# A graph network on one core: a shorter last destination block, scales taken ahead, column statistics beside the additions

## The reference, cut to what matters

```python
def _sage_bn_relu(h, src, dst, Wl, bl, Wr, gamma, beta):
    agg = segment_sum(h[src], dst, num_segments=N)
    deg = segment_sum(ones, dst, num_segments=N)
    mean_agg = agg / maximum(deg, 1.0)[:, None]
    out = mean_agg @ Wl + bl + h @ Wr
    mu = out.mean(axis=0); var = out.var(axis=0)
    out = (out - mu) * rsqrt(var + EPS) * gamma + beta
    return relu(out)
h = layernorm(x)
for params in three_layers:        # widths 256 -> 512 -> 512 -> 256
    h = _sage_bn_relu(h, src, dst, *params)
x = x + h
...
```

## Time and profile before

| what | value |
|---|---|
| median of 3 runs | 3179.72 us (3179.55 to 3182.9) |
| the profiled execution | 3180.59 us, span of its instructions 3178.8 us |
| TensorE (PE) busy | 2346.3 us, 74% |
| TensorE weight loads (PEld) busy | 1819.8 us, 57% |
| VectorE (DVE) busy | 1310.3 us, 41% |
| GpSimd (POOL) busy | 908.5 us, 29% |
| ScalarE (ACT) busy | 410.4 us, 13% |
| mean granted TensorE clock | 0.863 |

### The profile page before, as it was taken

The page is one execution under the profiler, slowest core; times in us unless marked ns, Lnnn a source line. Parts: engine busy times, 40 slices in busy tenths (PEclk is TensorE's granted clock), DMA queues, the critical chain, the costliest instruction groups (busy, mean ns, idle before and its releaser), DMA issues.

```text
span 3178.8 us, 40745 instructions
## 1 busy us (share of the span) xinstructions
PE 2346.3 (74%) x14330; PEld 1819.8 (57%) x14330; DVE 1310.3 (41%) x2751; ACT 410.4 (13%) x822; POOL 908.5 (29%) x643
## 2 busy tenths in 40 slices
PE   1122100058858999998996977999899995999997
PEld 1111100035636776776773455888688874888886
DVE  6599999954422011112116834113311775111111
ACT  0011000000005200004102213000200001322322
POOL 2588888888800000000002210000100000333332
PEclk6556555579979999999997969999999986999998
DMA  9833333367660699960251000444244424666665
GB/s 353 294 43 52 48 46 53 40 207 254 159 219 14 153 234 277 202 178 0 94 186 37 0 0 0 145 146 154 73 132 147 143 76 137 187 189 180 192 189 135
DMA packets 288646, 426.61 MB, mean 134 GB/s; under 512 B 166210, under 2 KB 223833, under 8 KB 288511
## 3 DMA queue, kind: packets, MB, share of 16 engines
q1 hardware_dynamic: 104959, 297.03, 28.9%
q10 hardware_dynamic: 109696, 106.77, 12.0%
q0 software_dynamic: 73936, 22.14, 8.0%
HBM read 307.61 MB, written 100.96 MB: 129 GB/s over the span
## 4 chain that ended last, share of the span: by engine, by line
PE 58%; DVE 7%; issue 3%; ACT 3%; DMA 1%; POOL 1%; DVEq 1%; ACTq 0%; SPq 0%
PE ps L1561 14%; PE ps L1778 7%; PE ps L1779 7%; PE ps L1856 7%; PE ps L1847 7%; PE ps L1499 4%; PE ps L1578 3%; PE ps L1729 1%; PE ps L1628 1%; PE ps L1756 1%; ACT harena L822 1%; DVE harena L1150 1%; DVE harena L1149 1%; DMA odd_counts<-harena 1%; DVE harena L1148 1%
## 5 line engine op out<-in xcount | busy, mean ns | idle before, releaser
L1778 PE MATMUL ps<-harena,ring 128*128 128x257 f16 x2500 | 555.3, 274 | 3.8 <-DVE harena L1237 2.7
L1779 PE MATMUL ps<-harena,ring 128*128 128x256 f16 x2500 | 554.9, 273 | 0.0
L1561 PE MATMUL ps<-ring,harena 128*128 128x320 f16 x4000 | 553.3, 301 | 1.9 <-issue 1.0
L1561 PEld LDWEIGHTS ps<-ring,harena 128*128 128x128 f16 x4000 | 393.6, 98 | 159.0 <-issue 3.6
L513 POOL DMA_INDIRECT at_counts<-harena x224 | 357.9, 1598 | 147.7 <-issue 66.7
L977 DVE SCALAR_TENSOR_TENSOR late<-ring,ps 128x1024 f16<-128x1024 f32 x312 | 379.0, 1276 | 2.7 <-issue 2.7
L1553 PE MATMUL ps<-ring,ones 128*128 128x320 f16 x250 | 44.7, 333 | 385.7 <-DVE ring L1057 385.7
L513 POOL DMA_INDIRECT odd_counts<-harena x192 | 307.6, 1602 | 60.3 <-issue 59.3
L1778 PEld LDWEIGHTS ps<-harena,ring 128*128 128x128 f16 x2500 | 242.8, 97 | 43.3 <-DVE harena L1281 3.9
L1779 PEld LDWEIGHTS ps<-harena,ring 128*128 128x128 f16 x2500 | 243.1, 97 | 32.4
L1553 PEld LDWEIGHTS ps<-ring,ones 128*128 128x128 f16 x250 | 26.3, 107 | 400.5 <-issue 388.2
(11 more groups left out here) (344 smaller groups left out, 2591.9 us busy)
## 6 DMA issues: line engine op xcount, KB each, us to landing
ring<-at_counts SPq DMA_DIRECT2D x150, 800.0 KB
ring<-L_ffn_W SPq DMA_DIRECT2D x64, 1024.0 KB, 5.5
ring<-ad_counts SPq DMA_DIRECT2D x50, 800.0 KB
ring<-key_rows SPq DMA_DIRECT2D x52, 512.0 KB
at_counts<-tarena ACTq DMA_DIRECT2D x5, 4000.0 KB
odd_counts<-tarena ACTq DMA_DIRECT2D x5, 4000.0 KB
xrows<-odd_counts SPq DMA_DIRECT2D x25, 800.0 KB
at_counts<-ring ACTq DMA_DIRECT2D x25, 800.0 KB
```

The costliest lines, as they stand in the source:

```text
L1561: ins = M(ps[:, 2 * f + h, 0:HB], part[:, t, (2 * k + f) * P:(2 * k + f + 1) * P], chunk[q][:, s, h * HB:(h + 1) * HB], start=(t == 0 and ...
L1778: M(ps[:, i, 0:F + 1], lhs, hh[:, t, 0:F + 1], start=(t == 0), stop=False)
L1779: ins = M(ps[:, i, 0:F], lhs, hl[:, t, :], start=False, stop=(t == T - 1))
```

## The change

- In the last block, the matmuls of aggregation, degree and Wr product that write the second half move `LAST` = 245 columns in place of 320. So does ScalarE's store of the Wr product. The inverse degrees of the 75 padded columns are set to zero by a memset. The matmuls with Wl keep 320 columns. The TensorE loops over blocks are peeled by one; layer 1's aggregation is written out for all five blocks, on TensorE and on VectorE.
- The scale of layer 1 is computed before layer 0's tables are summed. That of layer 2 is computed during layer 1's aggregation: the norm's VectorE part after block 0, its matmul after chunk 1 of block 1, its square root on ScalarE after 8 of the 25 turns; the scale's two matmuls after chunks 1 and 2 of block 2. Each scale has columns of its own.
- The statistics of one group of 128 columns follow the addition of the next.

```diff
+LAST = N - (NB - 1) * BC - HB
+SCOL = 340
...
-            def half_done(l, b, h):
+            def half_done(l, b, h, c=HB):
...
                 if l == 1:
-                    turn_adjacency(0, NB * NB)
+                    turn_adjacency(0, NB + 3)
+                    wait(c_sum, 1)
+                    nc.scalar.activation(w3norm, ps[:, 7, SCOL - 1:SCOL], ACT.Sqrt, scale=float(HID)).then_inc(c_norm, 1)
+                    turn_adjacency(NB + 3, NB * NB)
                 bn_sqrt(2 + l, nfo)
-                if l == 1:
-                    wait(c_sum, 1)
-                    nc.scalar.activation(w3norm, ps[:, 7, 200:201], ACT.Sqrt, scale=float(HID)).then_inc(c_norm, 1)
...
+                def column_stats(b, fo, width):
+                    dve.wait_ge(odone, b * nfo + (fo + 2))
+                    for h in range(2):
+                        c = HB if h == 0 else width
+                        o.mark(V.bn_stats(bn_st[:, fo, bass.ds(b * 2 + h, 1), :].rearrange("p a s -> p (a s)"),
+                                          tfeat[:, fo, bass.ds(b * BC + h * HB, c)]))
...
+                        if b == NB - 1:
+                            step(V.memset(deginv[:, N:], 0.0))
...
-                    for fo in range(nfo):
-                        dve.wait_ge(odone, b * nfo + (fo + 2))
...
+                        if fo >= 1:
+                            column_stats(b, fo - 1, width)
+                    column_stats(b, nfo - 1, width)
...
                 if l == 0:
+                    dve.wait_ge(w0_in, 16 * 11)
+                    bn_bound(0)
+                    half_scale(1, 4)
...
+                elif l == 1:
+                    aggregated(0, HB)
+                    o.settle()
                     dve.wait_ge(w2_in, 32)
                     V.scalar_tensor_tensor(out=feat[:, :, :].rearrange("p a b -> p (a b)")[:, 0:1024], in0=wr[:, 1024:2048], scalar=1.0, in1=wr[:, 1024:2048],
                                            op0=ALU.mult, op1=ALU.mult, accum_out=w3square).then_inc(c_square, 1)
                     dve.wait_ge(c_square, 1)
+                    aggregated(1, HB)
+                    dve.wait_ge(c_norm, 1)
+                    bn_bound(1)
+                    step(V.tensor_scalar(amax[:, 0:4], amax[:, 0:4], w3norm, None, ALU.mult))
+                    half_scale(2, 4)
+                    for b in range(2, NB - 1):
+                        aggregated(b, HB)
...
                         for part in (hh, hl):
-                            for h in range(2):
-                                ins = M(ps[:, 2 * f + h, 0:HB], part[:, t, (2 * k + f) * P:(2 * k + f + 1) * P], chunk[q][:, s, h * HB:(h + 1) * HB],
+                            for h, c in ((0, HB), (1, last)):
+                                ins = M(ps[:, 2 * f + h, 0:c], part[:, t, (2 * k + f) * P:(2 * k + f + 1) * P], chunk[q][:, s, h * HB:h * HB + c],
                                         start=(t == 0 and part is hh), stop=(t == T - 1 and part is hl))
...
                     ins.then_inc(chunk_used[q], 1)
+                    between(q)
...
-            with pe.Fori(0, NB) as b:
-                aggregate(1, b, 0, HID)
-                aggregate(1, b, 1, HID)
+            def next_square(q):
+                if q == 1:
+                    pe.wait_ge(w2_in, 32)
+                    pe.wait_ge(c_square, 1)
+                    M(ps[:, 7, SCOL - 1:SCOL], ones[:, :], w3square, start=True, stop=True).then_inc(c_sum, 1)
+            def next_scale(q):
+                if q == 1:
+                    scale_across(2)
+                elif q == 2:
+                    scale_spread(2)
+            for b in range(NB):
+                last = LAST if b == NB - 1 else HB
+                aggregate(1, b, 0, HID, last, next_square if b == 1 else next_scale if b == 2 else nothing_between)
+                aggregate(1, b, 1, HID, last)
+                if b == 1:
+                    pe.wait_ge(c_norm, 1)
                 mean_products(1, b, 4, 4)
```

More of the change, by code:

```diff
@@ L738, in enter_block @@
                     high_rows(b, (4,))
-                    half_done(l, b, 1)
+                    half_done(l, b, 1, LAST if last else HB)
                 half_relu(l, 0, 0)
@@ L930, in half_scale @@
             def half_scale(k, cols):
-                V.tensor_reduce(sc[:, 2:3], amax[:, 0:cols], AX.X, ALU.max).then_inc(sc_col, 1)
+                own = scale_of(k)
+                V.tensor_reduce(own[:, 2:3], amax[:, 0:cols], AX.X, ALU.max).then_inc(sc_col, 1)
                 dve.wait_ge(sc_row, k)
-                step(V.tensor_reduce(sc1[:, 0:1], ps[0:1, 7, 0:P], AX.X, ALU.max))
+                step(V.tensor_reduce(sc1[:, 0:1], ps[0:1, 7, SCOL:SCOL + P], AX.X, ALU.max))
                 step(V.tensor_scalar(sc1[:, 1:2], sc1[:, 0:1], 1e-30, None, ALU.max))
@@ L937, in half_scale @@
                 dve.wait_ge(sc_all, k)
-                step(V.tensor_scalar(sc[:, 1:2], ps[:, 7, P:P + 1], 2.0 ** -13, None, ALU.mult))
-                V.reciprocal(sc[:, 0:1], sc[:, 1:2]).then_inc(sc_ready, 1)
+                step(V.tensor_scalar(own[:, 1:2], ps[:, 7, SCOL + P:SCOL + P + 1], 2.0 ** -13, None, ALU.mult))
+                V.reciprocal(own[:, 0:1], own[:, 1:2]).then_inc(sc_ready, 1)
             def bn_bound(l):
@@ L1074, in _ @@
                     dve.wait_ge(c_square, 1)
+                    aggregated(1, HB)
[5 more added lines that the diff above has]
+                        aggregated(b, HB)
+                else:
+                    with o.loop(NB - 1, 2 * nfo) as b:
+                        aggregated(b, HB)
+                aggregated(NB - 1, LAST)
+                o.settle()
                 for fo in range(nfo):
@@ L1509, in enter_block @@
                         tile_rows(i)
-                    half_products(l, b, h, weights)
+                    half_products(l, b, h, weights, HB if h == 0 else last)
             pe.wait_ge(keys_dve, 3)
@@ L1530, in _, with nothing_between, aggregate @@
                 products(b)
-            def aggregate(l, b, k, width, at_rows=None):
+            def nothing_between(q):
+                pass
+            def aggregate(l, b, k, width, last=HB, between=nothing_between):
                 n = b * PASSES[l] + (FIRST[l] + k)
@@ L1551, in aggregate @@
                                 for j in range(BT):
-                                    for h in range(2):
-                                        ins = M(ps[:, 4 + h, 0:HB], ones16[:, :], chunk[q][:, j, h * HB:(h + 1) * HB],
+                                    for h, c in ((0, HB), (1, last)):
+                                        ins = M(ps[:, 4 + h, 0:c], ones16[:, :], chunk[q][:, j, h * HB:h * HB + c],
                                                 start=(t + j == 0), stop=(t + j == T - 1))
@@ L1580, in mean_products, with scale_across, scale_spread @@
                     ins.then_inc(ops, 1)
+            def scale_across(k):
+                pe.wait_ge(sc_col, k)
+                M(ps[0:1, 7, SCOL:SCOL + P], scale_of(k)[:, 2:3], ident[:, :], start=True, stop=True).then_inc(sc_row, 1)
+            def scale_spread(k):
+                pe.wait_ge(sc_pow, k)
+                M(ps[:, 7, SCOL + P:SCOL + P + 1], ones[0:1, :], sc1[:, 2:3], start=True, stop=True).then_inc(sc_all, 1)
             def half_scale(k):
[L1583 to L1586, removed]
+                scale_across(k)
+                scale_spread(k)
             pe.wait_ge(ent[0][1], T + 1)
@@ L1606, in turned_rows @@
                 ins.then_inc(ent[1][3], 1)
-            with pe.Fori(0, NB) as b:
+            with pe.Fori(0, NB - 1) as b:
                 enter_block(1, b, turned_rows, wr2)
+            enter_block(1, NB - 1, turned_rows, wr2, LAST)
             pe.wait_ge(lo, T + 1)
```

53 lines of the change are left out of this document (20 added, 33 removed).

## The result

| | before | after |
|---|---|---|
| median | 3181.69 us (6 executions, 3179.55 to 3182.9) | 3155.19 us (6 executions, 3152.72 to 3180.33) |
| ratio after / before | | 0.9936, 95% interval 0.9921 to 0.9952 |
| profiled execution | 3180.59 us | 3173.5 us |

The changed kernel is faster by 26.5 us in the median, but its times form two groups: four executions lie between 3152.7 and 3155.5 us, two at 3173.5 and 3180.3 us. The kernel before has no such second group. The profiled execution is one of the long ones, so its page shows what made it long. Here are its span and the chain that ended last (shares by engine, then by line).

What follows compares the result with a forecast made beforehand. TensorE's matmul stream and the gaps between layers were taken as the bound; 15.7 + 4.1 + 6.1 + 1.3 - 1.3 - 0.2 = 25.7 us saved, median 3154.0 us, range 3149.5 to 3160.5.

Steps and rivals of the forecast that it cites:

- The step that failed: Layer 1, ScalarE's queue: wait reached at 1157.3 us after eight turns, DMA queue not held, root 37 us early; no cost.
- The rival on written-out code: Layer 1's copied instructions starve TensorE: 3186 us at 8 us a copy (2%), or 3158 to 3166 us milder (4%).
- Columns: Last blocks' 245-column aggregation and Wr matmuls, plus stores, in layers 0 to 2: 15.7 us saved, 31 ns per aggregation matmul.
- Rival 2: Shortened aggregation matmuls wait for weight load or next chunk, saving nothing: 12.6 us lost, 3166.6 us; chance 5%.
- Layer 0 to the start of the Wl product: Layer 0's last block: shortened chunks save 3.3 us, less 0.2 us for zeroing the padded inverse degrees.
- Statistics: Ends of layers 0 and 1: only two calls stay behind the last addition, 2.05 us saved each, 4.1 us together.
- Scales: Ready before `bn_done`, so ReLU follows at once: 2.96 us saved in layer 0, 3.14 in layer 1, 6.1 together.
- Norm: End of layer 1: the norm's VectorE part leaves the path, 1.3 us saved.
- Small matmuls: Three fp32 matmuls entering TensorE's layer 1 stream cost 1.3 us, between bounds of 0.3 and 2.2 us.
- rival 4: Layer 1's small fp32 matmuls drain the fp16 stream, 1.5 us each, 3 us over the sum: 3157 us; chance 5%.
- Memset: Zeroing 75 columns on layer 0's path, between two VectorE steps, costs 0.2 us.
- Rival 1: Clock stays up across the shortened 6.8 us gaps after layers 0 and 1: 4.3 us more saved, 3149.7 us; chance 5%.

Runs made afterwards that it cites:

- the runs with 50 turns: Kernels before and changed, looped or written out, with the 25 table turns done twice; changed-schedule means 3317.7 us with loops, 3346.8 us with TensorE's code written out.
- the trace of the common group: A second trace of the changed kernel, unchanged, that fell into the shorter group of executions; span 3154.3 us.
- late_turns: Changed kernel with the last five of 25 table turns moved to layer 2, behind layer 1's square root; 3148.62 to 3157.7 us, ratio 0.9908.
- after_third: The changed kernel run again without any edit, on another chip; 3153.3 to 3159.91 us in four executions, ratio 0.991.

## Why the prediction was right or wrong

The median, 3155.19 us, is 1.2 us from the forecast. The mean over the executions, as the ratio has it, is 3161.3 us and lies outside my range, since about one execution in four is 16 to 25 us longer.

**The step that failed** is the one on ScalarE's queue: "ScalarE reaches its wait at 1157.3, after the eighth turn, so its DMA queue behind it isn't held, and the root is there 37 us before TensorE's wait". I asked what the new wait does to the turns, and whether the norm's root is early enough. I didn't ask what stands behind the turns: layer 1's own square root, on the path. The sum has no term for it, that is, it puts it at nothing; in the profiled execution it was 15.5 us. Before, the turns took 312 us of 371 in the one trace I had, last store included. I took this for a fixed length; it is a draw from a wide spread (250 to 376 us between first and last issue for one kernel), and the change narrows the room by 8 us while its written-out code, by the runs with 50 turns, lengthens the mean. The 8 us alone can't be the cause: an execution 16 to 25 us too long would, with 8 us more of room, still be 8 to 17 us too long, and the kernel before has none such in 57. The quoted sentence fails in a smaller way too: in the trace of the common group ScalarE is at its wait at 1136.7, before TensorE's small matmul, and its queue is held until 1141.1; there it cost nothing. That the turns hold the root in the profiled execution is shown by its rows; that taking turns away from ahead of the root removes the wait, by the trace of late_turns. That the other three long executions have the same cause is supported by the ten executions with fewer turns, but none of the three has a trace.

The rival on written-out code had the right culprit and the wrong victim. TensorE isn't starved: in the trace of the common group a written-out pass of 400 matmuls still takes 54.35 us. The Trainium skill (Runtime: NRT & Kernel Launch, Instruction fetch mechanics) says that page fetches are mostly hidden and unrolling is preferred. For TensorE, which runs the code, the rows agree (54.35 us looped and written out); what the fetches do to DMA transposes beside them the page leaves open, and here the means above point to a cost.

Point by point, in the trace of the common group:

- Columns: 6.17 us in layer 1 and 3.08 in layer 2, as said (6.2, 3.1). 200 shortened matmuls save 6.17 us, 30.9 ns each, so one of 245 columns takes 105.0 ns. Rival 2 is out; neither weight load nor chunk holds it.
- Layer 0 to the start of the Wl product: 906.53 to 940.47, 33.94 us against 37.90, 4.0 us where I had 3.3 less 0.2. Each chunk gave 0.78; most of the rest is luck, a shorter low-clock phase in the first chunk (7.70 us, 1.7 over the others; before 9.22, 2.4 over).
- Statistics: mis-sized. I said two calls stay behind the last addition. The statistics of a group follow the next group's addition, so the last two groups' calls, four in all, stand behind it: 1.43 us instead of 2.85, 1.4 us saved in each layer and not 2.05. That I could have read in the diff.
- Scales: 3.03 and 3.22 us, as said (2.96, 3.14). Norm: 1.3 us, as said.
- Small matmuls: 0.12 + 0.31 + 0.31 = 0.74 us, and the four blocks together became 0.99 us longer (1057.15 to 1349.52 against 1066.81 to 1358.19), below my 1.3, so rival 4 is out. Memset 0.12.
- Missed: the Wl product of layer 0 runs 1.66 us longer; this is the clock, see the last section. The Wr product behind layer 0's gap takes 10.64 us against 9.73, and the 16 instructions behind layer 1's 6.19 against 5.84. How long the clock stays low after a gap is mostly chance: the former took 9.06 to 10.66 us in the fourteen traces with the changed layer 0. Rival 1 is out: the gaps are 7.3 us, and the granted clock is 0.50 in both (958.0 to 963.0 and 1419.0 to 1423.0).

From the first degree matmul to layer 3's ReLU this makes 767.8 - 744.8 = 23.1 us (before rounding), against 25.7 forecast. So even in the common case 2.6 us of the sum were missing: 1.7 of the Wl product, 1.3 of the statistics and 1.3 behind the gaps, less what came out better. The medians hide it, since the tables happened to come 1.5 us earlier in that trace: that the median lies so near the forecast is partly luck.

## What to carry to other kernels

Before shortening a path, list for every engine what stands ahead of its next operation on that path, DMA issues with their waits included, and compare their length with the room that is left. One trace gives one draw of a contended transfer: with 59 us of slack in one execution it isn't known to be safe. Don't let a short operation that is on the path stand behind housekeeping of uncertain length in the same queue: a part of the housekeeping can go to a later stage, as in late_turns. And keep a loop where nothing is gained by writing it out.

## What the runs showed of the hardware

The clock of TensorE could fall in an idle time of only 2.15 us. In layer 0 TensorE now finishes its last matmuls earlier, while VectorE's reciprocal is as long as it was, so the pause ahead of the Wl product grew from 1.51 to 2.15 us. The windows of the trace of the common group (us, busy and count by engine, clock, DMA, GB/s):

```profile
938.00:941.00 3.00, 0.85 (x4) 0.51 (x3) 2.29 (x4) 0.00 (x0) 0.00 (x0) 0.90 1.01 420
941.00:944.00 3.00, 3.00 (x7) 1.86 (x6) 0.00 (x0) 0.00 (x0) 0.00 (x0) 0.53 1.02 425
944.00:946.00 2.00, 2.00 (x9) 1.37 (x9) 0.83 (x1) 0.00 (x0) 0.00 (x0) 1.00 0.77 323
```

The granted clock is at its lower level (1.2 of 2.4 GHz) for some 3 us though TensorE is busy again, and 32 instructions take 10.53 us instead of 8.87. In the trace of before it stayed up there (1.00 from 943 to 948). The length of the pause alone doesn't decide it, though. Of fourteen traces with the changed layer 0 the product takes 10.53 to 10.59 us in thirteen, but 8.89 us in that of after_third, the same kernel with the same pause of 2.15 us, where the clock stayed up:

```profile
941.00:944.00 3.00, 2.62 (x10) 1.91 (x11) 0.49 (x2) 0.00 (x0) 0.00 (x0) 1.00 1.02 429
```

So making an engine finish sooner than what it waits for can cost part of the gain.

Behind the aggregation, undisturbed, a turn of the table takes 8.0 us (1420.18 to 1428.15 in the first trace after). Beside the aggregation most took 8 to 16 us, but single turns took 20 to 41 us, three in the trace before and seven in the first trace after. Each moves the same 800 KB.
